# The read-out of a recurrence by fours instead of pairs, with the stages placed anew

## The reference

```python
def step(s, rkvw):
    r_t, k_t, v_t, w_t = rkvw
    a = k_t[..., :, None] * v_t[..., None, :]
    out = jnp.einsum('bhi,bhij->bhj', r_t, u * a + s)
    s = a + w_t[..., :, None] * s
    return (s, out)
```

## Time and profile before

| what | value |
|---|---|
| runs | 1798.56, 1798.26, 1789.37 us; median 1798.26 |
| the profiled execution: its time | 1787.11 us |
| its span | 1785.3 us |
| PE busy | 1584.3 us, 89% |
| DVE busy | 1222.6 us, 68% |
| ACT busy | 939.4 us, 53% |
| POOL busy | 769.4 us, 43% |

### The profile page before, as it was taken

One profiled execution on the slowest core, in us unless ns is written; L12 is line 12 of the kernel. 1 busy time (PEld: TensorE's weight loads), 2 busy tenths in 40 slices (PEclk: granted clock), 3 DMA queues, 4 the chain that ended last, 5 costly groups with the idle time before them and its releaser, 6 DMA issues.

```text
span 1785.3 us, 35476 instructions
## 1 busy us (share of the span) xinstructions
PE 1584.3 (89%) x13831; PEld 1027.2 (58%) x13831; DVE 1222.6 (68%) x2259; ACT 939.4 (53%) x1922; POOL 769.4 (43%) x882
## 2 busy tenths in 40 slices
PE   5898998899998999898988989889999899989856
PEld 3666555565565755655556655566556565566524
DVE  4743579655795658946699457975579566894496
ACT  4444555555655545556455565555565554564413
POOL 5632248503584146821478024860458314682000
PEclk9999999999999999999999999999999999999978
DMA  6001024200341005210061102420034100520060
GB/s 190 9 1 39 1 25 54 40 23 8 37 56 37 20 1 62 37 31 20 1 73 26 30 20 25 53 51 17 4 39 53 37 20 1 64 35 1 14 92 17
DMA packets 75923, 60.83 MB, mean 34 GB/s; under 512 B 39264, under 2 KB 60912, under 8 KB 75760
## 3 DMA queue, kind: packets, MB, share of 16 engines
q1 hardware_dynamic: 58000, 47.99, 18.6%
q10 hardware_dynamic: 17216, 10.55, 2.1%
q0 software_dynamic: 544, 0.03, 0.0%
HBM read 20.28 MB, written 4.19 MB: 14 GB/s over the span
## 4 chain that ended last, share of the span: by engine, by line
PE 63%; DVE 15%; ACT 10%; issue 6%; POOL 5%; ACTq 1%; DMA 0%; DVEq 0%; SPq 0%; POOLq 0%
PE bank L690 24%; PE bank L834 7%; PE bank L1097 6%; DVE late L1410 5%; PE bank L1034 5%; PE bank L706 3%; PE bank L1059 2%; DVE late L1422 2%; PE bank L967 2%; POOL soft_ring L1786 2%; PE bank L849 2%; PE bank L943 2%; PE bank L774 2%; ACT soft_ring L1250 2%; POOL late L1739 1%
## 5 line engine op out<-in xcount | busy, mean ns | idle before, releaser
L1786 POOL TENSOR_TENSOR soft_ring<-soft_ring,seg_max 128x512 f32<-128x512 f32 x256 | 285.5, 1127 | 259.2 <-DVE seg_max L1576 257.9
L1250 ACT ACTIVATE soft_ring<-soft_ring 128x512 f32<-128x512 f32 x256 | 160.5, 627 | 212.7 <-POOL soft_ring L1786 212.2
L1410 DVE TENSOR_TENSOR_SCAN late<-late 128x520 f32<-128x520 f32 (+1 forms) x128 | 204.7, 1599 | 3.7
L1739 POOL TENSOR_TENSOR late<-late 128x520 f32<-128x520 f32 x112 | 175.4, 1566 | 39.2 <-DVE late L1410 38.4
L1034 PE MATMUL bank<-ident,soft_ring 128*128 128x128 f32 x1024 | 160.6, 284 | 24.3 <-ACT soft_ring L1250 21.7
L1034 PEld LDWEIGHTS bank<-ident,soft_ring 128*128 128x128 f32 x1024 | 111.9, 141 | 102.0 <-ACT soft_ring L1250 47.8
L1576 DVE TENSOR_REDUCE seg_max<-soft_ring 128x8 f32<-128x512 f32 (+1 forms) x256 | 166.5, 674 | 0.2
L1752 POOL COPY late<-edge 128x8 f32<-128x8 f32 (+1 forms) x16 | 3.2, 198 | 336.6 <-DVE late L1514 288.5
L834 PE MATMUL bank<-early 32*128 32x128 f32 (+2 forms) x1024 | 144.5, 402 | 1.3 <-DVE soft_ring L1561 1.1
L1125 ACT ACTIVATE late<-bank 128x512 f32<-128x512 f32 (+4 forms) x103 | 57.9, 571 | 120.8 <-PE bank L690 118.7
L1794 POOL TENSOR_SCALAR soft_ring<-soft_ring,rden 128x256 f32<-128x256 f32 x64 | 59.3, 929 | 139.9 <-DVE rden L1538 139.9
(11 more groups left out here) (327 smaller groups left out, 3417.5 us busy)
## 6 DMA issues: line engine op xcount, KB each, us to landing
late<-late SPq DMA_DIRECT2D x112, 260.0 KB, 4.4
c<-in_ctx ACTq DMA_DIRECT2D x8, 512.0 KB, 4.0
x<-in_x ACTq DMA_DIRECT2D x8, 512.0 KB, 4.9
out_x<-late SPq DMA_DIRECT2D x7, 512.0 KB, 2.9
late<-late SPq DMA_DIRECT2D x16, 130.0 KB, 3.7
early<-early SPq DMA_DIRECT2D x16, 130.0 KB, 3.9
mask<-in_mask_Bx1xSxS_ff ACTq DMA_DIRECT2D x16, 128.0 KB, 4.0
mask<-in_mask_BxS_ik SPq DMA_DIRECT2D x8, 256.0 KB, 3.5
```

The source lines that it names most:

```text
L1250: af(soft[:, u % SOFT, :], soft[:, u % SOFT, :], ACT.Exp).then_inc(sig("exp"), 1)
L1410: nc.vector.tensor_tensor_scan(P.sj[:, n % 2, :], P.wP[:, k, :, :].rearrange("p b t -> p (b t)"), P.aj[:, n % 2, :], 0.0, ALU.mult, ALU.ad ...
L1739: tt(P.aj[:, n % 2, :], P.kP[:, k, :, :].rearrange("p b t -> p (b t)"), P.vj[:, n % P.depth, :], ALU.mult).then_inc(mine("kv_done"), 1)
L1786: tt(s, s, seg_max[:, u % SOFT, 0:segs].unsqueeze(2).broadcast_to([128, segs, 512 // segs]), ALU.subtract).then_inc(sig("sub"), 1)
```

## The change

Four rounds are collected before PE reads them out: rounds j = 0 to 3 and 4 to 7 of each half of the features, as four products side by side, each with its own 32 columns of result. The quad of rounds n - 3 to n is put into scan stage n + 2 (before: the pair into stage n + 3). DVE's read n with n % 4 == 0 waits for the whole quad before it. RS stays 4. All places of layer 3 are new.

```diff
         PLACES = {
-            "moments": (0, 0, 0, 0),
-            "normalize": (4, 5, 1, 0),
-            "turn": (11, 10, 3, 0),
-            "shift": (11, 10, 11, 9),
-            "maa": (15, 15, 15, 10),
+            "moments": (4, 0, 0, 0),
+            "normalize": (6, 8, 2, 3),
+            "turn": (7, 8, 5, 3),
+            "shift": (10, 8, 8, 4),
+            "maa": (14, 13, 15, 8),
...
-            "bonus": (56, 50, 53, 54),
-            "center": (125, 125, 121, 118),
-            "variance": (127, 127, 124, 126),
-            "gate": (130, 129, 124, 126),
-            "project": (133, 133, 124, 126),
+            "bonus": (56, 48, 57, 56),
+            "center": (129, 127, 125, 132),
+            "variance": (130, 130, 125, 133),
+            "gate": (133, 131, 127, 136),
+            "project": (133, 132, 128, 136),
...
         SCAN_PLACES = (
-            (63, 52, 64, 58), (63, 54, 67, 65), (64, 54, 67, 66), (65, 61, 67, 67), (71, 61, 69, 67),
-            (75, 79, 69, 67), (75, 79, 71, 67), (83, 89, 83, 67), (83, 90, 88, 85), (96, 93, 88, 89),
-            (100, 93, 100, 90), (105, 99, 106, 100), (109, 100, 108, 105), (112, 102, 109, 105), (112, 102, 115, 105),
-            (112, 106, 117, 105), (116, 107, 120, 110), (116, 110, 120, 110), (125, 115, 121, 110),
+            (66, 48, 64, 57), (66, 48, 66, 64), (66, 55, 67, 64), (70, 56, 68, 64), (71, 65, 68, 64),
+            (72, 87, 69, 64), (92, 89, 73, 64), (93, 92, 83, 67), (93, 95, 88, 85), (94, 99, 91, 92),
+            (112, 99, 100, 93), (112, 99, 106, 100), (112, 99, 108, 105), (112, 107, 112, 105), (115, 107, 114, 108),
+            (127, 108, 122, 108), (127, 111, 124, 115), (129, 119, 124, 121), (129, 121, 125, 127),
         )
...
-                        n = stage[1] - 3
-                        if 0 <= n < KT * HS and n % 2 == 1:
+                        n = stage[1] - 2
+                        if 0 <= n < KT * HS and n % RS == RS - 1:
                             k, j = n // HS, n % HS
-                            if j == 1:
+                            if j == RS - 1:
                                 t, full = fill(pe, P.hold, own("o3", k))
                             else:
                                 b, c = spot(own("o3", k))
                                 t, full = banks[b], sig(f"bank{b}_full")
                             pe.wait_ge(mine("rs_ready"), so_far("rs_ready") + n + 1)
-                            for i in (j - 1, j):
+                            for i in range(j - RS + 1, j + 1):
...
-                        if n >= RS and n % 2 == 0:
-                            pair = (n - RS) // 2
-                            if pair % 4 == 3:
-                                filled(own("o3", pair // 4))
-                            else:
-                                dve.wait_ge(mine("rs_used"), so_far("rs_used") + 3 * (pair // 4) + pair % 4 + 1)
+                        if n >= RS and n % HS == 0:
+                            filled(own("o3", n // HS - 1))
+                        elif n % RS == 0 and n:
+                            dve.wait_ge(mine("rs_used"), so_far("rs_used") + n // HS + 1)
```

More of the change, by code:

```diff
@@ L477, in build @@
         PLACES = {
-            "moments": (0, 0, 0, 0),
-            "normalize": (4, 5, 1, 0),
-            "turn": (11, 10, 3, 0),
-            "shift": (11, 10, 11, 9),
-            "maa": (15, 15, 15, 10),
[L483 to L494, removed]
-            "bonus": (56, 50, 53, 54),
-            "center": (125, 125, 121, 118),
-            "variance": (127, 127, 124, 126),
-            "gate": (130, 129, 124, 126),
-            "project": (133, 133, 124, 126),
-            "moments 2": (133, 133, 127, 126),
-            "normalize 2": (134, 133, 127, 134),
-            "turn 2": (134, 133, 127, 134),
@@ L503, in build @@
[L503 to L506, removed]
+            "moments": (4, 0, 0, 0),
[3 more added lines that the diff above has]
+            "maa": (14, 13, 15, 8),
+            "mix 0": (18, 29, 19, 13),
+            "mix 1": (21, 29, 20, 31),
+            "td": (29, 32, 28, 32),
+            "k": (34, 34, 34, 35),
@@ new lines, in build @@
+            "mix 2": (37, 37, 36, 37),
+            "decay": (44, 40, 42, 46),
+            "v": (44, 40, 42, 46),
+            "mix 3": (44, 40, 42, 47),
+            "mix 4": (46, 40, 42, 47),
+            "r": (46, 43, 44, 51),
+            "g": (49, 48, 50, 55),
+            "r u k": (50, 48, 50, 55),
+            "bonus": (56, 48, 57, 56),
[3 more added lines that the diff above has]
+            "project": (133, 132, 128, 136),
@@ L507, in build @@
+            "moments 2": (133, 133, 130, 136),
+            "normalize 2": (133, 133, 130, 137),
+            "turn 2": (134, 133, 130, 137),
+            "shift 2": (138, 143, 130, 145),
+            "ffn k": (145, 144, 140, 146),
+            "ffn r": (145, 146, 140, 153),
+            "ffn v": (148, 151, 149, 158),
         }
         SCAN_PLACES = (
[4 rows of a table removed]
[4 rows of a table added]
         )
@@ L535, in build @@
             aj_ready=16, edge3_ready=1, edge4_ready=1, kk_ready=2, kv_done=16,
-            oc_ready=2, ogT_ready=2, out_ready=4, rgn_ready=2, rs_ready=16, rs_used=6, rstd3_ready=1, rstd4_ready=1,
+            oc_ready=2, ogT_ready=2, out_ready=4, rgn_ready=2, rs_ready=16, rs_used=2, rstd3_ready=1, rstd4_ready=1,
             ruk_ready=2, s0_in=32, sj_ready=16, stats3_ready=1, stats4_ready=1, stored=16,
```

## The result

The changed kernel takes **1815.22 us** (median of 4 runs, 1813.24 to 1822.26); the kernel before took 1797.82 us (4 runs, 1789.37 to 1798.56). The ratio on record is 1.0122 [1.0092, 1.0152], 1.2% slower; these two medians alone give 1.0097. The kernel before was run again beside every experiment: those 43 executions took 1785 to 1807 us, the shortest at a mean granted clock of 0.983, the longest at 0.968. The one profiled for the rows of before had 0.983 too. The forecast was 1770, with 1752 to 1790 as the range. The profiled execution took 1815.97 us.

What follows compares the result with a forecast made beforehand. PE, busy 89%, was taken to bound most of each period; terms summed to -3.7, taken as -3.4 us, -24 over seven groups, +1 tail: -23. From both ends, 1764 and 1775, the middle 1770 us was stated, range 1752 to 1790.

Steps and rivals of the forecast that it cites:

- A quad costs a pair: Read-out on PE (L774): four column strips run side by side, so a quad takes 0.99 us, a pair 0.98.
- Rival C: Read-out: four strips don't overlap in 512-column passes, a quad takes 1.84 us; about 1786 or no change; chance 0.06.
- (a): Scan before layer 2's waiting transpose: PE work saved there gives 0, an earlier scan 1 gives -0.3 us a period.
- (d): Outside the scan: layer 3's moved flips give -0.5 us a period (0 to -1.0); other moved places are covered by PE's backlog.
- turn: Layer 3's flips (L698, 0.98 us), moved on PE from place 11 to 7, fill a wait for POOL: -0.5 us.
- (b): Scan behind layer 2's waiting transpose: six pairs become three quads on PE, -2.9 us a period.
- (c): Two later pairs' waits for DVE, at places 116 and 125: the first goes, -0.5 us; the second counts 0.
- Rival A: PE's waits end with partner engines, which take the saving; about 1783, or 1793 if all is taken; chance 0.14.
- (e): DVE's new waits for quads: read 8 costs 0 to 3.1 us, taken as +0.5; heads(1) waits under 0.82.
- Rival B: Scan: DVE waits for quads and PE for DVE, making it slower, up to 1823 on the profiled level; chance 0.08.
- In the periods it stays at 1.00 either way: PE's granted clock in the whole periods: full before and after the change, so no cost.
- The tail: Last block, DVE-bound: PE's saving is covered, a later clock rise costs +1 us (bounds -1 and +7).

Runs made afterwards that it cites:

- e8: The changed kernel with the old places for all stages ahead of the scan, up to the bonus; 1812.84 us, ratio 1.0104.
- e3: The changed kernel plus three unread 512-column products per whole period, on PE at places 67, 69 and 78; 1824.87 us, ratio 1.0185.
- e13: The changed kernel plus six unread 512-column products a period, on PE at 69, 71, 78 and 83; 1810.42 us, ratio 1.0102.
- e6: The kernel before with pairs for the first four rounds and quads behind them, at PE 90, 112 and 125; 1815.21 us, ratio 1.0131.
- e2: The kernel before with quads at the old places, except PE's scan stages 9 (96 to 92) and 17 (116 to 125); 1859.92 us, ratio 1.0376.
- e15: The kernel before plus 24 unread 256-column products on PE in its last block; 1793.07 us against 1792.22, ratio 0.9993.
- e9: The kernel before with each pair's products cut to 64 of 512 columns in the seven whole periods; 1807.28 us, ratio 1.0073.
- e10: The kernel before with each pair's products issued twice in the seven whole periods; 1810.06 us, ratio 1.0090.

## Why the prediction was wrong

- **A quad costs a pair (right).** 1.00 us at full clock, L774 at 31.6 us. Rival C is out.
- **(a), "quad 0 waits for read 3, about as pair 0 waited", and the other places of (d) counted as covered (the first step that failed).** The forecast up to layer 2's first scores was -0.3 for an earlier scan and -0.5 for "turn". "Turn" did what was said: PE reaches layer 0's first projection 21.8 us into its period, before 22.5. The rest did not. Read 3 starts 97.8 us into the period, before 97.0; quad 0 starts at 98.6, where pair 0 started at 92.1 and its wait was 1.21 us, now 1.88; the waits around it are 1.51 and 1.06. The first scores come 2.2 us later, at full clock. Half of that stands with the places ahead of the scan (e8). Which stage's place costs which part wasn't tried.
- **(b), "six pairs become three quads: -2.9", and (c), -0.5 (failed).** The timeline showed PE without waits from 725.5 to 752.2, and I took work in that stretch for time. But a stretch without waits is not one without slack at its end. Behind the first scores the period is at full clock as long as before (108.4 us in e3 and e13, 109.0 in e8, against 108.7). Rival A's mechanism was true there, and I had given it 0.14. How much of it is slack of the partners and how much new waits for quads stays open: e6, with the same saving, has both.
- **(e) (right at read 8, wrong at heads(1)).** In the changed kernel read 8 waits 1.17 us, inside its bounds 0 to 3.1. But heads(1) was to wait less than 0.82 us, and waits 6.72 for the last quad, which now stands at PE 129 (the line is below the list). That costs PE little: DVE's next long waits shrink (11.58 to 7.33 us for ACT, 6.90 to 2.09 for PE), and PE waits 0.30 us for what follows. Rival B's mechanism is real, 3.03 us at read 4 and 5.91 at read 8, once the quads stand at the old places (e2).
- **"In the periods it stays at 1.00 either way" (failed).** The lower clock was granted for 6.8 to 13.7 us of each period, 10.8 in the mean; the profiled execution of before had 1.1, but e15 shows the same periods with 0 to 10.2. I had seen the mechanism in the tail, and did not ask whether a PE with 4 us less to do would keep 1.00 in the rest.
- **The sum.** Forecast was 211.7 less 3.4. At full clock the changed kernel's period is, by e3 and e13, about 213.7: 2.0 us longer. The lower clock adds 1.7 to it in the mean and had added 0.3 before. So, by this estimate, the new places lost 2.0 of the 3.4 us, the clock 1.4, and the quads' saving arrived nowhere. At e3's price (0.33 to 0.43 us for each) the 9.7 us more at the lower clock would be 3.2 to 4.2 us and would leave the places nothing; the first part of the period, 2.2 us longer at full clock, shows that this is too much.
- **The tail.** Together with the last whole period it grew by 6.8 us; forecast +1, bounds up to +7. In the tail itself the low stretch is 41.0 us, before 34.1. What each of the two is worth in this end wasn't tried on the changed kernel; e15 shows more clock in the old tail to be worth nothing.

```profile
788.58 0.69 DVE L1427 TENSOR_TENSOR late<-bank,late 128x512 f32<-128x512 f32 x1 [6.72 <-PE bank L774]
```

The Trainium skill has the rule I should have weighed. "TensorE: Matmul & The Clock Gate", "A second HAM failure mode", tells of a kernel whose TensorE idles in short gaps between groups of products, often enough for the clock to go back and forth. The trace agrees in kind: the clock fell to 0.50 in a period whose PE waits were at most 1.88 us long ahead of the fall, with PE busy 91% of the whole.

**What stays open.** Which PE gaps decide: the kernel before has a wait of 2.38 us and, in five of six periods of that trace, no fall, and periods of one kernel with the same work (e3, e6, e15) fall or don't. What the changed kernel itself would take at full clock: it showed no such period, and 213.7 is that of e3 and e13, with unread products in it. Whether other places would let the quads gain: no version tried did, and none beat the kernel before.

## What to carry to other kernels

An engine that is busy 90% of the time need not be the bound: make the operation in question shorter, and twice as long, each in one experiment, before costing its removal at its full time. Cut a period at two or three landmarks and compare the parts in periods at the same granted clock: a part that is longer by the same amount in every period is the schedule's, one that varies from period to period is the clock's. On TensorE look at the granted clock of every stretch: less work can bring the lower clock. And where buffers are handed back in larger lots (four rounds in place of two), look at both waits at every place: the producer's for the buffers (read 8 in e2) and the consumer's for the last of the lot (quad 0 here).

## What had not been expected of the hardware

- Taking about 5.6 us of a period's products off TensorE made the program 0.7% slower, at a granted clock of 0.96 for 1.00 (e9); adding 6.8 us kept it at 1.00 (e10).
- One kernel's periods, of the same instructions, took from 213.7 to 219.6 us with 0 to 13.7 us at the lower clock (e3): a spread of 2.8% within one execution.
- Four products of 512 columns on four strips of 32 columns took 1.00 us, two took 0.98.
